# Gated FFN with routed experts: token tiles taken in groups of four, with z and the raw weights held once

## The chip, the cores and the metric

The kernel runs on one core of a Trainium2 chip, as one program. The metric is the device time of one execution in microseconds (us). Three executions of the kernel before took 4530.27, 4531.44 and 4532.99 us, so the median is 4531.44 us.

## What is computed

```python
x = x + tanh(g_xattn[0]) * mixer(ctx, ctx, layernorm(x))      # causal convolution of k v pairs, 64 heads of 8
x = x + tanh(g_ffn[0]) * ffn(layernorm(x))
def ffn(x):                                  # T = 8192 tokens, D = 1024, F = 512, E = 7 experts
    shared = (x1 * silu(x2)) @ shared_w2     # x1, x2 = split(x @ shared_w1)
    aff  = sigmoid(x @ gate_w + expert_bias) # two best experts of a token: mask
    sel  = top_k(where(mask, aff, -1).T, capacity)            # capacity = T // E = 1170 per expert
    out  = _ffn(x[sel], routed_w1, routed_w2) * w             # w = aff where kept, else 0
    return shared + zeros.at[sel].add(out)
```

All of it is in float32. TensorE is fed float32r, whose values are rounded, so each factor is split into a high and a low part, and a product is three matmuls: high x high, high x low, low x high.

## The kernel before, in words

Three blocks follow one another, each behind a barrier. `prepare_filters` is short. `gated_conv` is the mixer: 64 steps, which also leave the normalized tokens in HBM both as rows (`z_d`) and transposed (`zT_d`), the residual in `out`, and the gate's logits in `logit_d`. `experts` is the FFN, and the change touches that block alone. Token tiles are 128 tokens wide for the shared expert (64 tiles) and 117 for a routed one (10 tiles of 117 slots, 7 experts).

**A group is two tiles** (`GS` = 32 shared groups, `GE` = 5 per expert). For each group PE makes the first product (`first_product`, lines 1336 to 1347): for each of four blocks `j` of F and for the two halves of `w1` (value and gate) it sums 8 chunks of D times 3 matmuls, 192 in all, whose moving side is z of the group, 256 or 234 columns. Then comes the second product of the group before (`second_product`, lines 1349 to 1365): for each tile and each half of D 12 matmuls of 512 columns, 48 in all. I call such 12 matmuls a half. An expert's last group is followed by its own second product too (`after`).

Around it, ACT makes Silu of the gate half (`swish`), the high part of the hidden tile (`high`) and of z (`split`); DVE makes the product (`gate_up`), the low parts (`low`, `split`) and takes the results out of PSUM (`result`, line 1266): for the shared expert y = tanh(g) * result + residual, in place in `y[t]`, and for a routed one the result times the weight of its slot. `zh`, `zl`, `hh`, `hl` exist twice, once for each of two groups in turn, so that the z of the next group is split during the first product of this one. PSUM holds `ps1` (two, one bank each), `ps2` (two, one per tile, two banks each) and `psT`.

**Orders written out by hand.** SP issues all loads and stores of the shared part in one queue: per group `load_z(k + 2)`, `store(k - 1)`, `residual(k)` (lines 889 to 892), where a residual waits until the store of the same `y[t]` has landed. POOL gathers a routed tile with an indirect DMA (`gather`, line 948), as rows that PE transposes (`turn`, line 1325), and adds a result tile into `out` with an indirect DMA (`scatter`, line 960), waiting for each to land before the next. Weights come through `raw`, 32 KB per partition: `w1` in four pairs of blocks (`load_pair`), then `w2` in the first half of the same buffer; each is split into high (ACT) and low (DVE) at the turn from one expert to the next (`w1_high`, `w1_low`, `w2_high`, `w2_low`).

**Routing** runs on DVE beside the shared groups. `make_scores` (line 1080) comes first, before the first product may begin. Then the capacity's threshold is searched over 30 bits (`find_bit`), one step in each block `j` of a group; PE adds the counts over the partitions (`tally`). Scans and numbering follow, up to `routed`. POOL then writes (token, weight) of each token's first and second choice into the list in HBM (`scatter_column`, line 928): 64 columns times two indirect DMAs, where each waits for the one before. The list is read back (line 945), and the gathers of the first expert can begin.

## Time and profile before

| | |
|---|---|
| median of 3 executions | 4531.44 us |
| the profiled execution, its own time | 4534.36 us |
| its span, first to last instruction | 4532.4 us |
| PE busy | 4433.4 us (98%), 33098 matmuls |
| PE weight loads busy | 4275.3 us (94%) |
| DVE busy | 2780.8 us (61%) |
| ACT busy | 1492.2 us (33%) |
| POOL busy | 881.7 us (19%) |
| granted PE clock, mean | 0.992 of 2.4 GHz |

The FFN's block begins at 2176.3 us of the span. A matmul's listed length holds its whole way through the array and overlaps with the next one's, so the rate of PE is to be read from the distance of two starts in the timeline. "SPq" is SP's queue of DMA issues; an issue of several DMAs in one row lasts from the first to the last, waits among them. In the groups of instructions, the idle time is that of the engine just before them, with what ended it.

### The profile page before, as it was taken

What the parts mean: (1) busy time and instruction counts of PE and PEld (TensorE: products, weight loads), DVE (VectorE), ACT (ScalarE), POOL (GpSimd) and SP (SyncE); (2) the same over time, 40 slices, a digit from 0 to 9 for tenths busy, and PEclk for the clock granted to TensorE, in tenths of its full rate; (3) what the DMA queues carried; (4) which work ended last, traced back from release to release, by engine and by line L of the source; (5) the groups of instructions that cost most, each with busy time, mean ns of one, the idle gap of its engine ahead of it and who ended that gap; (6) DMA issues with size and microseconds to landing.
All of it is one profiled execution on the core that took longest, in us unless ns stands there. A gap on an engine that the chain in (4) does not pass through costs nothing.

```text
span 4532.4 us, 85207 instructions
## 1 busy us (share of the span) xinstructions
PE 4433.4 (98%) x33098; PEld 4275.3 (94%) x33098; DVE 2780.8 (61%) x3215; ACT 1492.2 (33%) x2179; POOL 881.7 (19%) x1065
## 2 busy tenths in 40 slices
PE   7999999999999999999699999999999999999998
PEld 7999999999999999999599999999999999999997
DVE  7999999999999999998544522222233233233232
ACT  4454554545455454554211111111122122122120
POOL 1222222122221222222000023322111111111211
PEclk9999999999999999999799999999999999999999
DMA  3333333333333333332533344334343443443432
GB/s 106 112 116 106 115 106 110 113 111 116 106 111 106 111 116 109 116 104 86 127 98 88 86 110 117 90 89 99 86 122 78 94 112 70 97 112 70 97 79 39
DMA packets 200325, 457.80 MB, mean 101 GB/s; under 512 B 31434, under 2 KB 97343, under 8 KB 200187
## 3 DMA queue, kind: packets, MB, share of 16 engines
q1 hardware_dynamic: 173515, 388.38, 29.9%
q0 software_dynamic: 26672, 67.34, 7.4%
q8 instruction: 116, 1.90, 0.2%
q14 instruction: 22, 0.18, 0.0%
HBM read 285.80 MB, written 169.83 MB: 101 GB/s over the span
## 4 chain that ended last, share of the span: by engine, by line
PE 50%; DVE 1%; DMA 1%; issue 0%; ACT 0%; POOL 0%; SPq 0%; POOLq 0%; ACTq 0%; DVEq 0%
PE moe_ps L1343 11%; PE moe_ps L1344 11%; PE moe_ps L1345 11%; PE moe_ps L1359 5%; PE moe_ps L1360 5%; PE moe_ps L1361 5%; PE moe_psT L1332 1%; DMA out<-moe_y,moe_add_i 0%; DMA moe_zin<-zT_d 0%; DVE moe_w1l L1232 0%; DVE moe_zl L1245 0%; DVE moe_raw L1146 0%; PE moe_psT L1368 0%; DVE moe_raw L1145 0%; ACT moe_zh L1013 0%
## 5 line engine op out<-in xcount | busy, mean ns | idle before, releaser
L568 PE MATMUL att_psY<-att_kv_hi,att_tz_hi 128*128 128x288 f32 x4608 | 1393.5, 302 | 30.6 <-DVE att_kv_lo L444 30.6
L569 PE MATMUL att_psY<-att_kv_lo,att_tz_hi 128*128 128x288 f32 x4608 | 1359.4, 295 | 0.0
L570 PE MATMUL att_psY<-att_kv_hi,att_tz_lo 128*128 128x288 f32 x4608 | 1355.9, 294 | 0.0
L1343 PE MATMUL moe_ps<-moe_zh,moe_w1h 128*128 128x234 f32 (+1 forms) x4288 | 1205.9, 281 | 30.1 <-DVE moe_zl L1245 25.5
L1344 PE MATMUL moe_ps<-moe_zl,moe_w1h 128*128 128x234 f32 (+1 forms) x4288 | 1199.0, 280 | 3.5 <-issue 3.5
L1345 PE MATMUL moe_ps<-moe_zh,moe_w1l 128*128 128x234 f32 (+1 forms) x4288 | 1198.6, 280 | 0.0
L568 PEld LDWEIGHTS att_psY<-att_kv_hi,att_tz_hi 128*128 128x128 f32 x4608 | 865.4, 188 | 30.6 <-issue 30.6
L570 PEld LDWEIGHTS att_psY<-att_kv_hi,att_tz_lo 128*128 128x128 f32 x4608 | 867.7, 188 | 0.0
L569 PEld LDWEIGHTS att_psY<-att_kv_lo,att_tz_hi 128*128 128x128 f32 x4608 | 867.6, 188 | 0.0
L1343 PEld LDWEIGHTS moe_ps<-moe_zh,moe_w1h 128*128 128x128 f32 x4288 | 824.9, 192 | 34.0 <-issue 31.3
L1344 PEld LDWEIGHTS moe_ps<-moe_zl,moe_w1h 128*128 128x128 f32 x4288 | 825.1, 192 | 6.2 <-issue 4.1
L1345 PEld LDWEIGHTS moe_ps<-moe_zh,moe_w1l 128*128 128x128 f32 x4288 | 825.1, 192 | 0.0
L1024 ACT ACTIVATE moe_act_s<-moe_ps 128x234 f32<-128x234 f32 (+1 forms) x268 | 100.5, 375 | 1744.2 <-PE moe_ps L1345 1744.2
L1258 DVE TENSOR_TENSOR moe_hid<-moe_ps,moe_act_s 128x234 f32<-128x234 f32 (+1 forms) x268 | 110.6, 413 | 886.7 <-ACT moe_act_s L1024 879.7
L343 ACT ACTIVATE att_y<-att_psY 128x576 f32<-128x576 f32 x512 | 333.4, 651 | 860.7 <-PE att_psY L570 858.9
L289 POOL TENSOR_TENSOR att_root<-att_mv,att_eps 128x1 f32<-128x1 f32 x128 | 183.2, 1431 | 1639.8 <-DVE att_mv L434 1560.9
L1359 PE MATMUL moe_ps<-moe_w2h,moe_hh 128*117 128x512 f32 (+1 forms) x1072 | 422.6, 394 | 0.0
L1360 PE MATMUL moe_ps<-moe_w2l,moe_hh 128*117 128x512 f32 (+1 forms) x1072 | 420.6, 392 | 0.0
L1361 PE MATMUL moe_ps<-moe_w2h,moe_hl 128*117 128x512 f32 (+1 forms) x1072 | 420.3, 392 | 0.0
L444 DVE TENSOR_TENSOR att_kv_lo<-att_kv,att_kv_hi 128x2304 fp32r<-128x2304 f32 x128 | 323.5, 2528 | 0.7 <-ACT att_kv_hi L336 0.7
L462 DVE TENSOR_TENSOR att_prod<-att_y,att_qx 128x2048 f32<-128x2048 f32 x128 | 293.6, 2294 | 6.1 <-ACT att_y L343 0.4
L475 DVE TENSOR_TENSOR att_prod<-att_prod 128x2048 f32<-128x2048 f32 x128 | 293.1, 2290 | 2.3
(155 smaller groups left out, 5167.1 us busy)
## 6 DMA issues: line engine op xcount, KB each, us to landing
att_kT<-in_cT SPq DMA_DIRECT2D x64, 512.0 KB, 4.0
att_xn<-in_x SPq DMA_DIRECT2D x64, 512.0 KB, 5.8
att_tz_hi<-filt_hi SPq DMA_DIRECT2D x64, 512.0 KB, 3.8
att_tz_lo<-filt_lo SPq DMA_DIRECT2D x64, 512.0 KB, 4.8
out<-att_x SPq DMA_DIRECT2D x64, 512.0 KB, 4.0
z_d<-att_z SPq DMA_DIRECT2D x64, 512.0 KB, 3.7
zT_d<-att_zT SPq DMA_DIRECT2D x64, 512.0 KB, 4.7
moe_zin<-zT_d SPq DMA_DIRECT2D x64, 512.0 KB
```

What stands on the lines that cost most here:

```text
L343: nc.scalar.activation(y[a // G][:, a % G].rearrange("p (c b) i -> p c (b i)", c=2), psY[a % 2][:, :, 0:NB * PAIRS], ACT.Copy).then_inc(y_ ...
L444: nc.vector.tensor_tensor(kv_lo[u][:, keys_of(half)].rearrange("p t b i -> p (t b i)"), kv[half][:, :, :, :].rearrange("p t b i -> p (t b ...
L462: nc.vector.tensor_tensor(place(0, [HD, D1 + 1], [1, HD]), near, runs(qx[u], half, 0, [1, D1 + 1], [1, HD]), ALU.mult)
L568: nc.tensor.matmul(acc, tz_hi[u][:, d:d + P], hi, start=(c == 0), stop=False)
L569: nc.tensor.matmul(acc, tz_hi[u][:, d:d + P], lo, start=False, stop=False)
L570: last = nc.tensor.matmul(acc, tz_lo[u][:, d:d + P], hi, start=False, stop=(c == a))
L1343: nc.tensor.matmul(acc, w1h[:, c, cols], zh[u][:, c, 0:2 * w], start=(c == 0), stop=False)
L1344: nc.tensor.matmul(acc, w1h[:, c, cols], zl[u][:, c, 0:2 * w], start=False, stop=False)
L1345: last = nc.tensor.matmul(acc, w1l[:, c, cols], zh[u][:, c, 0:2 * w], start=False, stop=(c == C - 1))
L1359: nc.tensor.matmul(acc, hh[u][:, f, rows], w2h[:, f, cols], start=(f == 0), stop=False)
L1360: nc.tensor.matmul(acc, hh[u][:, f, rows], w2l[:, f, cols], start=False, stop=False)
L1361: last = nc.tensor.matmul(acc, hl[u][:, f, rows], w2h[:, f, cols], start=False, stop=(f == FC - 1))
```

## The change

The FFN takes tiles in groups of four in the shared expert (16 groups of 512 tokens) and of four, three and three in a routed one (468, 351 and 351 tokens), so `ps1` becomes two tiles of two banks, and `ps2` one set of two banks instead of two sets. The odd width 351 is rounded up to 352. `zh` and `zl` exist once; a group's z is split after the first product of the group before has ended, in a *window*: there PE makes the second-product halves of the previous group and, in the routed part, turns the tiles of the next one between them, in an order that `window` gives to PE and DVE alike. `zin`, `y`, `hh`, `hl` stay two. `act_s` and `hid` become one each. The gate half of a block is now made before the value half, and Silu starts after it. `raw` is halved to 16 KB per partition: pairs 0 and 1 of `w1` lie in its halves, pairs 2 and 3 follow when 0 and 1 are split. The list exists in two copies, one for each token's first choice and one for its second; each scatter waits only for the previous one of its own copy, and the two are added after they are read back. `make_scores` is done by DVE inside the first group, after block 0, and two routing steps follow each of the blocks 0 to 2 of the next seven groups. The cut diff:

```diff
-    GE = 5
-    M = slots // (2 * GE)
-    TILES = E * 2 * GE
-    GS = H // 2
+    PARTS = (4, 3, 3)
+    PER = sum(PARTS)
+    NG = len(PARTS)
+    M = slots // PER
+    TILES = E * PER
+    GT = 4
+    GS = H // GT
...
+    list_of = [list_d, nc.dram_tensor("list_e", (E * slots + P, 2), I32).ap()]
+    def rows_of(n):
+        return list_of[n][0:E * slots, :].rearrange("(r q) c -> q r c", q=M)
...
-        raw = m.sb("raw", [P, C * F2])
+        raw = m.sb("raw", [P, FC * D])
+        raw1 = [raw[:, q * C * 2 * P:(q + 1) * C * 2 * P].rearrange("p (c b f) -> p c b f", c=C, b=2) for q in range(2)]
...
+        zh = m.sb("zh", [P, C, GT * P], F32R)
+        zl = m.sb("zl", [P, C, GT * P], F32R)
+        act_s = m.sb("act_s", [P, GT * P])
+        hid = m.sb("hid", [P, GT * P])
...
-        ps1 = [m.ps(f"ps1_{j}", [P, 2, 2 * P]) for j in range(2)]
-        ps2 = [m.ps(f"ps2_{t}", [P, 2, BANK]) for t in range(2)]
+        ps1 = [m.ps(f"ps1_{j}", [P, 2, BANK]) for j in range(2)]
+        ps2 = m.ps("ps2", [P, 2, BANK])
...
+        PLACES = [["scores"]] + [STEPS[a:a + EACH] for a in range(0, len(STEPS), EACH)] + [[]]
+        LEAD = len(PLACES)
...
+            lead = [shared(k) for k in range(LEAD)]
+            row(lead, None, shared(LEAD))
+            with eng.Fori(LEAD // 2, GS // 2 - 1) as p:
+                row(pair(2 * p + 1), shared(2 * p)._replace(u=0), shared(2 * p + 3)._replace(u=1))
+            firsts = expert_groups(1, 0)
+            row([shared(GS - 1), *firsts], shared(GS - 2), expert_groups(2, 1)[0])
+            with eng.Fori(0, (E - 3) // 2) as q:
+                both = expert_groups(2 * q + 2, 1) + expert_groups(2 * q + 3, 0)
+                row(both, expert_groups(2 * q + 1, 0)[-1], expert_groups(2 * q + 4, 1)[0])
+            ends = expert_groups(E - 1, 1) + expert_groups(E, 0)
+            row(ends, expert_groups(E - 2, 0)[-1], None)
...
+        def window(prev, nxt):
+            halves = [("half", t, b) for t in range(prev.nt) for b in range(2)] if prev else []
+            tiles = nxt.nt if nxt else 0
+            order = []
+            for a in range(max(len(halves), 1)):
+                order += [("tile", t, None) for t in range(tiles) if t * max(len(halves), 1) // tiles == a]
+                order += halves[a:a + 1]
+            return order
...
+                if j < 2:
+                    wait(sp, w2h_set, FC * n)
+                    wait(sp, w2l_set, FC * n)
+                else:
+                    sp.wait_ge(w1h_set, 2 * FC * n + 2 * (j - 1))
+                    sp.wait_ge(w1l_set, 2 * FC * n + 2 * (j - 1))
...
+            load_z(0, 0)
+            load_pair(0, 0, shared_w1[0])
+            load_z(0, 1)
             sp.dma_start(logit, logit_d).then_inc(logit_in, 16)
             sp.dma_start(g[:, :], g_ffn.rearrange("(a e) -> a e", a=1).to_broadcast([P, 1])).then_inc(const, 16)
-            load_z(0)
-            load_w1(0, shared_w1[0])
-            sp.wait_ge(list_made, 2)
-            sp.dma_start(list_d[0:E * slots, :].rearrange("(r q) c -> q r c", q=M), lists[:, :, :]).then_inc(list_init, 16)
+            load_pair(0, 1, shared_w1[0])
+            load_z(0, 2)
+            load_z(0, 3)
+            load_pair(0, 2, shared_w1[0])
+            load_pair(0, 3, shared_w1[0])
+            load_z(1, 0)
+            load_z(1, 1)
+            sp.wait_ge(list_made, 4)
+            for n in range(2):
+                sp.dma_start(rows_of(n), lists[0][:, :, :].bitcast(I32)).then_inc(list_init, 16)
             load_w2(0, shared_w2[0])
...
             def shared_rows(k):
-                load_z(k + 2)
-                store(k - 1)
-                residual(k)
-            with sp.Fori(1, GR + 4) as k:
+                load_z(k + 1, 2)
+                load_z(k + 1, 3)
+                store(k - 1, 0)
+                residual(k - 1, 2)
+                store(k - 1, 1)
+                residual(k - 1, 3)
+                load_z(k + 2, 0)
+                load_z(k + 2, 1)
+                store(k - 1, 2)
+                residual(k, 0)
+                store(k - 1, 3)
+                residual(k, 1)
...
             def scatter_column(h):
                 for n in range(2):
+                    wait(pool, scattered[n], h * 16)
+                    pool.sem_inc(passed, 1)
                     nc.gpsimd.tensor_copy(stage_i[n][:, :], slot_of[:, bass.ds(h, 1), n:n + 1].rearrange("p a b -> p (a b)")).then_inc(staged, 1)
                     nc.gpsimd.tensor_copy(stage_p[n][:, :], pay[:, bass.ds(h, 1), n, :].rearrange("p a b -> p (a b)")).then_inc(staged, 1)
                     pool.wait_ge(staged, h * 4 + (2 * n + 2))
                     pool.sem_inc(passed, 1)
-                    wait(pool, scattered[1 - n], h * 16 + 16 * n)
-                    pool.sem_inc(passed, 1)
-                    nc.gpsimd.indirect_dma_start(list_d, bass.IndirectOffsetOnAxis(stage_i[n][:, 0:1], 0),
+                    nc.gpsimd.indirect_dma_start(list_of[n], bass.IndirectOffsetOnAxis(stage_i[n][:, 0:1], 0),
                                                  stage_p[n][:, :], None).then_inc(scattered[n], 16)
...
+            for n in range(2):
+                pool.wait_ge(scattered[n], 16 * H)
+                pool.dma_start(lists[n][:, :, :].bitcast(I32), rows_of(n)).then_inc(list_in, 16)
+            pool.wait_ge(list_in, 32)
...
+            def rows(back, ahead, beyond):
+                for t in range(2, ahead.nt if ahead else 0):
+                    gather(ahead, t)
+                for t in range(back.nt if back else 0):
+                    scatter(back, t)
+                for t in range(2 if beyond else 0):
+                    gather(beyond, t)
...
+            def group(prev, cur, nxt):
+                for j in range(FC):
+                    swish(cur, j)
+                    if cur.i == 1 and j == 0:
+                        for c in range(FC):
+                            w2_high(cur, c)
+                    high(cur, j)
+                if nxt:
+                    act.wait_ge(up, FC * cur.k + FC)
+                    for t in range(nxt.nt):
+                        split(nxt, t)
+                        if turnover(cur, nxt) and t == 1:
+                            w1_high(nxt.n, 0)
+                    if turnover(cur, nxt):
+                        for j in range(1, FC):
+                            w1_high(nxt.n, j)
...
+            def group(prev, cur, nxt):
+                places = PLACES[cur.k] if cur.kind == "shared" and isinstance(cur.k, int) and cur.k < LEAD else []
                 for j in range(FC):
-                    gate_up(k, j, w)
-                    if next_kind and j % 2 == 0:
-                        split(k + 1, 1 - u, j // 2, next_kind)
-                    low(k, u, j, w)
-                    if first:
-                        w2_low(n, j)
-                    if places:
-                        route(places[j])
-                if not first:
-                    turnover = next_kind == "routed" and (kind == "shared" or i == GE - 1)
-                    results(k - 1, kind, n + 1, list(range(FC)) if turnover else [])
-            def after_shared():
-                results(GS - 1, "shared", 1, list(range(FC, 2 * FC)))
-                dve.wait_ge(list_in, 16)
-                nc.vector.tensor_scalar(scale[:, :], lists[:, :, 1].bitcast(F32), tg[0:M, 0:1], None,
-                                        ALU.mult).then_inc(scaled, 1)
-                dve.wait_ge(scaled, 1)
-            def after(n, k, u, last):
-                results(k, "routed", n + 1, [] if last else list(range(FC, 2 * FC)))
-            make_scores()
+                    gate_up(cur, j)
+                    low(cur, j)
+                    if cur.i == 1 and j == 0:
+                        for c in range(FC):
+                            w2_low(cur, c)
+                    for step in places[2 * j:2 * j + 2]:
+                        route(step)
+                if cur.kind == "routed" and isinstance(cur.n, int) and cur.n == 1 and cur.i == 1:
+                    weights_listed()
+                turning = turnover(cur, nxt)
+                for what, t, half in window(prev, nxt):
+                    if what == "tile":
+                        split(nxt, t)
+                        if turning and t == 1:
+                            w1_low(nxt.n, 0)
+                        if turning and t == nxt.nt - 1:
+                            w1_low(nxt.n, 1)
+                    else:
+                        result(prev, t, half)
+                if turning:
+                    for j in range(2, FC):
+                        w1_low(nxt.n, j)
...
+                wait(pe, y_set, 2 * (grp.tile + t) + (half - 1))
...
+            def group(prev, cur, nxt):
+                places = PLACES[cur.k] if cur.kind == "shared" and isinstance(cur.k, int) and cur.k < LEAD else []
+                pe.wait_ge(zh_set, cur.tile + cur.nt)
+                pe.wait_ge(zl_set, cur.tile + cur.nt)
+                left = list(places)
                 for j in range(FC):
-                    if isinstance(i, int) and i == 0:
-                        pe.wait_ge(w1h_set, 2 * FC * n + 2 * (j + 1))
-                        pe.wait_ge(w1l_set, 2 * FC * n + 2 * (j + 1))
-                    first_product(k, u, j, w)
-                    if places and j > 0:
-                        sum_partitions(places[j - 1])
-                    if next_kind == "routed" and j % 2 == 0:
-                        turn(k + 1, j // 2)
-                if not (isinstance(i, int) and i == 0):
-                    if i == 1:
-                        pe.wait_ge(w2h_set, FC * n + FC)
-                        pe.wait_ge(w2l_set, FC * n + FC)
-                    second_product(k - 1, 1 - u, w, places[FC - 1] if places else None)
-            def after_shared():
-                second_product(GS - 1, 1, P)
-            def after(n, k, u, last):
-                second_product(k, u, M)
+                    if cur.i == 0:
+                        pe.wait_ge(w1h_set, 2 * FC * cur.n + 2 * (j + 1))
+                        pe.wait_ge(w1l_set, 2 * FC * cur.n + 2 * (j + 1))
+                    wait(pe, gated, FC * cur.k + (j - 1))
+                    for b in (1, 0):
+                        first_product(cur, j, b)
+                        if j > 0 and left:
+                            sum_partitions(left.pop(0))
+                for what, t, half in window(prev, nxt):
+                    if what == "tile":
+                        if nxt.kind == "routed":
+                            turn(nxt, t)
+                    else:
+                        second_product(prev, t, half)
```

`first_product(grp, j, b)` now makes one half `b` of a block with the group's width, `second_product(grp, t, half)` one half. `load_z(k, t)` waits for `zh_set` and `zl_set` to reach 4k + t - 1, `residual(k, t)` for the last store of `y[t % 2]`. At the end SP stores groups 14 and 15 of the shared part without z loads ahead, and loads pairs 2 and 3 and `w2` of the first expert between them. POOL calls `rows` once per group.

## Rows read from the trace of the kernel before

**Rows 1.** Busy time in stretches: length, PE busy, granted clock, DMA share, GB/s

```profile
2176.29:2199.10 22.81, 0.00 (x0) 0.50 1.10 242
2199.10:2253.93 54.83, 50.43 (x387) 0.90 0.60 116
2719.96:2787.80 67.84, 67.84 (x482) 1.00 0.52 124
3314.79:3486.30 171.51, 171.51 (x1282) 1.00 0.38 90
4491.80:4532.40 40.60, 22.84 (x101) 0.82 0.31 48
```

**Rows 2.** Groups of PE matmuls by line and shape: busy, mean ns, idle

```profile
L1343 PE MATMUL moe_ps<-moe_zh,moe_w1h 128*128 128x234 f32 x2240 | 622.7, 278 | 0.2 <-issue 0.2
...
L1343 PE MATMUL moe_ps<-moe_zh,moe_w1h 128*128 128x256 f32 x2048 | 583.2, 285 | 29.9 <-DVE moe_zl L1245 25.5 <-DVE moe_hid L1258 4.4
```

**Rows 3.** Timeline of PE, first product of two shared tiles: start, length

```profile
2699.89 0.28 PE L1343 MATMUL moe_ps<-moe_zh,moe_w1h 128*128 128x256 f32 x1
...
2701.33 0.28 PE L1343 MATMUL moe_ps<-moe_zh,moe_w1h 128*128 128x256 f32 x1
```

**Rows 4.** Timeline of PE, second product of a shared tile

```profile
2744.67 0.39 PE L1361 MATMUL moe_ps<-moe_w2h,moe_hl 128*128 128x512 f32 x1
...
2745.58 0.39 PE L1359 MATMUL moe_ps<-moe_w2h,moe_hh 128*128 128x512 f32 x1
```

**Rows 5.** Timeline of PE, first product of two routed tiles

```profile
3319.81 0.27 PE L1343 MATMUL moe_ps<-moe_zh,moe_w1h 128*128 128x234 f32 x1
...
3320.70 0.27 PE L1345 MATMUL moe_ps<-moe_zh,moe_w1l 128*128 128x234 f32 x1
```

**Rows 6.** Timeline of PE: the first product of the FFN begins

```profile
2199.11 0.55 PE L1343 MATMUL moe_ps<-moe_zh,moe_w1h 128*128 128x256 f32 x1 [25.46 <-DVE moe_zl L1245]
```

**Rows 7.** Chain that ended last, from 2170 us: start, length, what

```profile
2206.36 12.21 DMA moe_zin<-zT_d
2218.59 1.06 ACT moe_zh L1013
2219.68 1.23 DVE moe_zl L1245
```

**Rows 8.** Timeline of DVE: last step of the scores

```profile
2193.62 0.62 DVE L1118 SCALAR_TENSOR_TENSOR moe_score<-moe_y,moe_score 128x448 f32<-128x448 f32 x1
```

**Rows 9.** Timeline of DVE, results of a shared group

```profile
2748.50 0.75 DVE L1271 SCALAR_TENSOR_TENSOR moe_y<-moe_ps,moe_tg,moe_y 128x512 f32<-128x512 f32 x1 [1.87 <-PE moe_ps L1361]
```

**Rows 10.** Timeline of the SP queue, stores and residual loads

```profile
2754.72 0.58 SPq L875 DMA_DIRECT2D out<-moe_y  x1
...
2760.60 0.58 SPq L870 DMA_DIRECT2D moe_y<-out  x1
...
2822.75 0.59 SPq L875 DMA_DIRECT2D out<-moe_y  x1
...
2827.96 0.59 SPq L870 DMA_DIRECT2D moe_y<-out  x1
```

**Rows 11.** DMA issues of the page: count, KB each, us from issue to landing

```profile
att_tz_hi<-filt_hi SPq DMA_DIRECT2D x64, 512.0 KB, 3.8
att_tz_lo<-filt_lo SPq DMA_DIRECT2D x64, 512.0 KB, 4.8
...
moe_zin<-z_d,moe_get_i POOLq DMA_INDIRECT x70, 4.7
```

**Rows 12.** Timeline of POOL: first scatter of the list, then loading the list

```profile
2610.67 0.19 POOL L930 COPY moe_stage_i<-moe_slot_of 128x1 int32<-128x1 int32 x1 [432.86 <-DVEq L1226]
...
3189.09 3.41 POOL L945 DMA_DIRECT2D moe_lists<-list_d  x1 [2.24 <-DMA list_d<-moe_stage_p,moe_stage_i]
```

**Rows 13.** Timeline of POOL at the end: scatters of results

```profile
4499.84 1.59 POOL L968 DMA_INDIRECT out<-moe_y,moe_add_i  x1 [0.86 <-POOL moe_add_i L965]
...
4507.50 1.57 POOL L968 DMA_INDIRECT out<-moe_y,moe_add_i  x1 [0.86 <-POOL moe_add_i L965]
```

More of the change, by code:

```diff
@@ new lines, in experts, with shared @@
+        STEPS = list(range(BITS)) + ["compare", "scan ties", "scan ties on", "keep", "scan kept", "scan kept on",
+                                     "number", "first", "second", "weigh", "no second", "no first"]
+        EACH = 2 * (FC - 1)
+        PLACES = [["scores"]] + [STEPS[a:a + EACH] for a in range(0, len(STEPS), EACH)] + [[]]
+        LEAD = len(PLACES)
+        assert LEAD == 9 and GS >= LEAD + 3 and (GS - 1 - LEAD) % 2 == 0
+        def shared(k):
+            return Grp("shared", k, GT * k, 0, GT, k % 2 if isinstance(k, int) else None, 0, k if isinstance(k, int) else 2)
@@ new lines, in routed_group, with expert_groups, schedule, row @@
+        def routed_group(n, k0, u0, i):
+            at = sum(PARTS[:i])
+            return Grp("routed", k0 + i, PER * (n - 1) + (H + at), at, PARTS[i], (u0 + i) % 2, n, i)
+        def expert_groups(n, u0):
+            return [routed_group(n, NG * (n - 1) + GS, u0, i) for i in range(NG)]
+        def schedule(eng, group):
+            def row(groups, before, behind):
+                chain = [before, *groups, behind]
+                for a in range(1, len(chain) - 1):
+                    group(chain[a - 1], chain[a], chain[a + 1])
+            def pair(k):
+                return [shared(k)._replace(u=1), shared(k + 1)._replace(u=0)]
+            lead = [shared(k) for k in range(LEAD)]
[9 more added lines that the diff above has]
+            row(ends, expert_groups(E - 2, 0)[-1], None)
@@ new lines, in rows, with around @@
+            def rows(back, ahead, beyond):
[5 more added lines that the diff above has]
+                    gather(beyond, t)
+            def around(groups, before, behind):
+                chain = [before, *groups, *behind]
+                for a in range(1, len(groups) + 1):
+                    rows(chain[a - 1], chain[a + 1], chain[a + 2])
@@ new lines, in after_next @@
+            def after_next(n):
+                return expert_groups(n + 1, 0)[0:2]
+            one = expert_groups(1, 0)
+            gather(one[0], 0)
+            gather(one[0], 1)
+            rows(None, one[0], one[1])
+            rows(None, one[1], one[2])
+            for t in range(2):
+                pool.wait_ge(stored[t], 16 * (GT // 2 * GS))
+            two = expert_groups(2, 0)
+            rows(one[0], one[2], two[0])
+            rows(one[1], two[0], two[1])
+            with pool.Fori(2, E) as n:
+                around(expert_groups(n, 0), expert_groups(n - 1, 0)[-1], after_next(n))
@@ L988, in _ @@
+            zero = shared(0)
+            split(zero, 0)
+            w1_high(0, 0)
+            for t in range(1, GT):
+                split(zero, t)
+            for j in range(1, FC):
+                w1_high(0, j)
             act.wait_ge(const, 16)
@@ L1055, in after_shared @@
-            def after_shared():
-                act.wait_ge(up, FC * GS)
-                w1_high(1)
-            def after(n, k, u, last):
-                if not last:
-                    act.wait_ge(up, FC * (k + 1))
-                    w1_high(n + 1)
-            split(0, 0, 0, "shared")
-            split(0, 0, 1, "shared")
-            w1_high(0)
-            schedule(act, group, after_shared, after)
+            schedule(act, group)
         @block.vector
@@ L1427, in build @@
+            pe.wait_ge(made, 2)
+            schedule(pe, group)
+            last = expert_groups(E, 0)[-1]
+            for t in range(last.nt):
+                for half in range(2):
+                    second_product(last, t, half)
 def build(nc, x, xT, cT, g_xattn, g_ffn, ssm_kernel, D, gate_w, expert_bias, shared_w1, shared_w2,
```

525 lines of the change are left out of this document (247 added, 278 removed).

## Prediction

> **What bounds the kernel now.** I began with the busy shares (PE 98%, DVE 61%, in the table above), then asked for stretches, since a share is a mean over two stages. Inside the FFN, PE is busy for the whole of a stretch of two shared groups (67.84 of 67.84 us) and of a whole expert (171.51 of 171.51) [rows 1]: no wait ends last there, so only shorter PE work can gain, and every new PE wait costs its full length. PE idles only around the edges: 25.5 us before the first product of the FFN and 4.4 us before its second group [rows 2], and at the end, where the last 40.6 us hold 22.84 us of PE work [rows 1].
>
> What does a matmul cost? Its listed length (278, 285 ns) overlaps the next, so I took the distance between starts. At 256 columns 12 starts take 1.44 us, 120.0 ns each [rows 3]; at 512 columns 4 take 0.91, 227 ns [rows 4]; at 234 columns 8 take 0.89, 111 ns [rows 5]. Columns at the granted 2.4 GHz explain 106.7, 213.3 and 97.5 ns. What is left is 13.3, 13.9 and 13.8 ns: a cost **per matmul**, whatever its width. The 512-column row is the second product; it is the only one of the width that the first product is to get.
>
> **First products.** Before, they are 3 x (2240 + 2048) matmuls [rows 2]. After, 16 shared groups and 21 routed ones, 192 each.
> - Shared, four tiles: before, the row of 67.84 us [rows 1]. After, 192 x 0.227 = 43.6 us and 96 second-product matmuls x 0.227 = 21.8 us: 65.4. Saved 2.4 x 16 = 39 us.
> - Routed, an expert: before 960 x 0.1113 = 106.8 us. After, 192 x (468/2.4 + 13.8 = 208.8 ns) = 40.1 us and 384 x (352/2.4 + 13.8 = 160.5 ns, as 351 is rounded up to 352) = 61.6: 101.7. Saved 5.1 x 7 = 36 us. Second products and transposes keep their number.
> Together **-75 us**.
>
> The Trainium skill (TensorE: Matmul & The Clock Gate, Back-to-back issue gap) gives N/2.4 + 2.5 ns for one matmul after another. That rule speaks against this change: by it 5760 fewer matmuls save 14 us, not 75. The rows above disagree at all three widths, and I go by them.
>
> **Start of the FFN, +5.** Scores leave the way of the first product, but four tiles of z must now be split before it. SP orders z, a pair of w1, z, the second pair, then z 2 and 3, each into a buffer that the split of z 0 or 1 frees. Counting 512 KB every 1.8 us behind the first landing near 2180 (an estimate from the landings around this stretch), the last z is there near 2194; ACT's and DVE's split take 1.06 and 1.23 us [rows 7], and PE starts at about 2196.5 instead of 2199.1 [rows 6]: -2.6. The scores took until 2194.2, 18 us after the stage began at 2176.3 [rows 1, 8]; now they run on DVE from 13 us into group 0, whose product lasts 44 us. They hold back the gate of block 1 until 31 us; block 3 asks for it at 33. Hidden, with 2 us to spare.
> Then a new hole: zh and zl exist once, so no split of group 1 can begin before group 0's product ends, there are no halves of a previous group to cover it, and z 2 and 3 are loaded only into freed buffers. Last gate and high 1.6 us, split of z 0 2.3: 3.9; load of z 2 4 to 5 (512 KB took 3.8, and 4.8 as the second of two [rows 11]); split of z 2 2.3, then that of z 3, which lands 2 us later. About 12.5 us idle, and 2 more at the lower clock level after it: this stage shows 0.50 granted while PE is idle and 0.90 in the stretch after [rows 1]. Against this stand the old 4.4 us hole and its own slow matmuls: 54.83 us for 384 matmuls of 120 ns, 46.1: 8.7 [rows 1]. Old offset 2199.1 + 8.7; new 2196.5 + 2 + 12.5 + 2: +5. The list is now written twice at the start, and behind the single write a z load took 12.2 us [rows 7]; by my count both writes and w2 are through at about 2246, when z 2 is asked for. So I allow up to +15, and down to 0.
>
> **Routing steps, +2.5.** Two steps now lie in a block of 10.9 us, as one did in 5.8. Four parts of w2l (1.23 us each, the size of the split [rows 7]) go in front of the first one: PE waits 3.3 us once. The tie scan holds PE about 1 us, and its old two stalls (under 2 us together) go, which takes 0.8 off. 0 to +6.
>
> **The shared window, +25.** This is my largest unknown. With PE at T (end of a group's product), PE makes eight halves of 2.72 us; y has two buffers for four tiles. So tile 2's first result needs: tile 0 stored, then its residual loaded. In SP's order two z loads stand ahead of that store, the second one waiting for the split of z 1, which DVE does after result 1. Result 1 ends 6.25 us after T (two halves, then 0.75 [rows 9]), the split of z 1 at 7.5, the second z load goes out, and the store at 7.9. Store to freed buffer, from the second store of a pair to the load that waits for it: 5.9 and 5.2 us [rows 10]; I take 5.1 from seven such pairs. Then the load, 3.9: 16.9; result 0.75 and semaphores 0.3: 18.1. PE wants to start half 6 at 16.3, and ps2 is one set, so half 6 waits for this result. PE loses 1.8 us. Who is behind: half 7, then the next group's product; z 3's split, at about 20, isn't later than that. Windows of that kind: groups 1 to 14, 14 x 1.8 = **25 us**. With 3.8 for both transfers next to nothing is lost; with 5.9 for both 4.3 us each, 60 us.
>
> **Routed windows, +4.** Here y is freed by scatters, 7.66 us from one to the next [rows 13]. The first goes out at about T + 8.6, tile 2's result comes at 15.5, tile 3's at 21.4 while its buffer is free at 22.5; PE waits only for results two halves back, so it isn't held. A gather goes out 1.1 us after its buffer is freed and takes 4.7 [rows 11]; tile 3 is turned 8 us later at the nearest. POOL's chain is 2 gathers, 4 scatters and 2 gathers, some 45 us in a 4-tile window of 55. Turn 1 waits for z 0's split about 0.2 us: 21 x 0.2 = 4. A new expert's w1 comes through two buffers: pair 0 is split by T + 9.5 (needed 20), pair 3 by 28 (needed 50). Cover if that fails: none. Bounds 0 and +15.
>
> **Lists, 0.** The old chain took 578 us for 128 scatters, 4.5 each [rows 12], every one waiting for the last. Two lists let one run beside the other; I reckon 6 us per pair, so 380 us. Routing now ends near 2700 instead of 2610, the lists are there near 3100, and the first turn asks for its gather near 3245. Price 0 as long as those 145 us last.
>
> **End, +4.** From the last product's end (2 matmuls into the last stretch) to the end of the program it is 40.3 us, for 22.3 us of halves [rows 1]. Now 6 scatters follow instead of 4: 40.3 + 2 x 7.66 = 55.6, for 33.5 us of halves. Overhang 22 instead of 18.
>
> **Sum.** -75 + 5 + 2.5 + 25 + 4 + 4 = -34.5. The profiled execution took 4534.4 us (span 4532.4): 4499.9. The median shown is 2.9 below it: **4497 us**.
>
> **Rivals.**
> - *The residuals come in time.* For it: 3.8 us is the shorter landing of the pair [rows 11], and the z load ahead may be over sooner. Then -25: 4472. Against: the second of two takes 4.8 there, and stores 5.2 and 5.9 [rows 10]. Chance 0.16.
> - *The residual chain costs its upper end*, as list scatters run beside it: 14 x 4.3 = 60 instead of 25: 4532, no change. 0.10.
> - *The list becomes the bound (slower).* If the two lists' scatters serialise after all in POOL's DMA queue, they take 578 us from 2700, loading both lists 33 more and a gather 6: turn 0 of the first expert at 3317 instead of 3245, and nothing else is there for PE. +72: 4569. It decides from about 7.9 us per pair (506 us for 64 pairs) against the old 9.0. For it: both lists go through POOL's one software queue. Against: 128 entries of 8 bytes are little to move, so most of the 4.5 us must be the way to completion, which two can share. 0.08.
> - *The change doesn't save per matmul*: wide first products would need more than their columns plus 13.8 ns, with only some 14 us gained: 4558. The second product at the same width speaks against it. 0.02.
> - Some wait that I don't see, of over 25 us: 0.08, mostly slower.
> The forecast keeps 0.56.
>
> **How the numbers follow.** A measurement of this kernel tells 0.2%, 9 us, from no change. Below 4522: forecast, first rival and a part of the second and last, 0.76; within 9 us 0.11; slower 0.13. The range takes the unknown costs' bounds: low 4497 - 25 - 5 - 4 = 4463; high 4497 + 35 + 8 = 4540, which leaves out the list case.
>
> **What would show it.** Distances of 227, 209 and 160 ns between first-product starts show the saving. In groups 1 to 14, PE idle before line-wise the second product of tile 2 or 3, put down to DVE's result and that to the residual's DMA, 1 to 3 us each, shows the window; none would show the first rival. One PE hole of 12 us between groups 0 and 1; POOL's last list scatter before 3120; six scatters 7.7 us apart at the end. PE idle before the first transposes in the list case. The forecast is wrong if idle time in the shared windows is near 0 or near 60 us, or if expert periods exceed 167 us by more than 1.

## The result: 4556.7 us, slower by half a per cent, and the profile after

| | before | after |
|---|---|---|
| median | 4531.44 us | 4556.7 us |
| lowest and highest of 5 runs | 4529.17 and 4534.48 | 4553.46 and 4557.42 |
| span of the profiled execution | 4532.4 us | 4555.4 us |
| PE busy | 4433.4 us, 33098 matmuls | 4385.9 us, 27338 matmuls |
| granted PE clock, mean | 0.992 | 0.984 |

The ratio is 1.0054, with a 95% interval of 1.0042 to 1.0065. The forecast was 4497 us, in a range of 4463 to 4540: the change was slower than all of it. PE is busy 47 us less, and the time still grew by 25.

**What came as forecast.** Two stretches of the changed kernel (length, then busy time of PE, PE weight loads, DVE, ACT and POOL, then granted clock, DMA share, GB/s). The first is one expert and answers to the 171.51 us of [rows 1]; the second holds two shared windows.

```profile
3520.10:3686.41 166.31, 166.31 (x897) 148.44 (x896) 53.45 (x66) 32.96 (x46) 31.58 (x40) 1.00 0.41 96
2720.00:2860.00 140.00, 128.91 (x550) 105.69 (x549) 39.67 (x61) 17.31 (x23) 52.73 (x117) 0.96 0.33 90
```

An expert takes 166.31 us, 5.2 less than before; 5.1 were forecast. In the shared part PE is no longer busy throughout: 128.91 of 140 us, at a clock of 0.96 instead of 1.00. Now the groups of PE matmuls, first product and then second product, each shared and routed (count, busy, mean ns, idle time before them), which answer to [rows 2]:

```profile
L1440 PE MATMUL moe_ps<-moe_zh,moe_w1h 128*128 128x512 f32 x1024 | 403.9, 394 | 33.4 <-DVE moe_zl L1338 21.8 <-issue 11.5
L1440 PE MATMUL moe_ps<-moe_zh,moe_w1h 128*128 128x352 f32 x896 | 289.3, 323 | 0.0
L1458 PE MATMUL moe_ps<-moe_w2h,moe_hh 128*128 128x512 f32 x512 | 213.0, 416 | 62.8 <-DVE moe_y L1365 62.8
L1458 PE MATMUL moe_ps<-moe_w2h,moe_hh 128*117 128x512 f32 x560 | 225.5, 403 | 3.3 <-DVE moe_y L1370 3.3
```

The hole between groups 0 and 1 is the 11.5 us of the first row (about 12.5 forecast). The new entry is 62.8 us ahead of the shared second product, ended by DVE's `result` (line 1365). DVE's own waits show that this line waits for a DMA (us in total, times, longest):

```profile
DVE moe_y L1365 <- DMA moe_y<-out: 183.2, 32, 9.7
```

It is one wait per window, 14 of them, always before half 6, the first half of tile 3: it needs the bank of PSUM that half 4 filled, and DVE can't empty that one before tile 2's residual is there. Three of the 14 in PE's timeline (in brackets the idle time): a typical one, the longest, and the last, which is also the shortest.

```profile
2398.25 0.50 PE L1458 MATMUL moe_ps<-moe_w2h,moe_hh 128*128 128x512 f32 x1 [3.56 <-DVE moe_y L1365]
...
2912.44 0.80 PE L1458 MATMUL moe_ps<-moe_w2h,moe_hh 128*128 128x512 f32 x1 [7.01 <-DVE moe_y L1365]
...
3273.23 0.79 PE L1458 MATMUL moe_ps<-moe_w2h,moe_hh 128*128 128x512 f32 x1 [2.94 <-DVE moe_y L1365]
```

What the first of these three is made of shows in the chain that ended last (start, length, what), here from the split of z 1 on. PE's product of the group had ended at 2378.1, which is the T of the prediction.

```profile
2384.52 1.23 DVE moe_zl L1338
...
2386.60 4.96 DMA out<-moe_y
...
2391.72 5.63 DMA moe_y<-out
...
2397.45 0.76 DVE moe_y L1365
...
2398.25 0.50 PE moe_ps L1458
```

The store goes out at T + 8.5 (7.9 forecast) and takes 5.0 (5.1 forecast); the residual load takes 5.6, not 3.9. The same two rows of the longest wait, which stands beside the list scatters:

```profile
2897.35 8.05 DMA out<-moe_y
...
2905.56 6.05 DMA moe_y<-out
```

Over the 14 windows the load takes 5.6 to 6.1 us in the eight away from the scatters and 5.7 to 6.6 in the six beside them; the store takes 4.4 to 5.4 and 5.9 to 8.1. Beside the scatters it is mainly the store that grows.

After the wait PE is slow for a while. These stretches of the typical window show it: the clock column falls from 1.00 to 0.71 and returns.

```profile
2384.00:2388.00 4.00, 4.00 (x20) 3.30 (x19) 2.49 (x3) 1.06 (x1) 0.00 (x0) 1.00 0.56 181
2396.00:2400.00 4.00, 1.75 (x6) 1.37 (x7) 2.54 (x3) 0.00 (x0) 0.00 (x0) 0.87 0.32 100
2400.00:2404.00 4.00, 4.00 (x14) 3.22 (x13) 0.38 (x1) 0.00 (x0) 0.00 (x0) 0.71 0.93 259
2404.00:2408.00 4.00, 4.00 (x20) 3.28 (x19) 1.12 (x2) 0.00 (x0) 0.00 (x0) 1.00 0.71 263
```

PE's timeline there gives the price. Two starts at the lower level (1.2 GHz), and two once the clock is back at 2.4 GHz:

```profile
2399.56 0.63 PE L1459 MATMUL moe_ps<-moe_w2l,moe_hh 128*128 128x512 f32 x1
2399.99 0.63 PE L1460 MATMUL moe_ps<-moe_w2h,moe_hl 128*128 128x512 f32 x1
...
2402.70 0.40 PE L1458 MATMUL moe_ps<-moe_w2h,moe_hh 128*128 128x512 f32 x1
2402.93 0.40 PE L1459 MATMUL moe_ps<-moe_w2l,moe_hh 128*128 128x512 f32 x1
```

Starts lie 0.43 us apart instead of 0.23, over some eight matmuls. I call *excess* what the distances of all starts in the 8 us behind a wait have above 0.227 us, summed: 1.75 us here, 1.44 to 2.78 in the 14 windows, 26.4 us together. About 0.12 us of each is there also behind a short wait at full clock (below), so the clock costs 25 us. **A window wait thus costs its idle time and about 1.8 us more: 62.8 + 24.7 = 87.5 us where 25 were forecast.** That surplus of 62.5 us is about the whole miss (60 us in the medians).

My theory then: the residual chain is longer than forecast, and each wait lowers the clock as well. Rivals: the list scatters beside it, a fixed cost of the wider groups, contention inside the chain.

### The profile page after: what moved, and what is told of

The parts are those of the page before. It is cut to its first block, busy times and chain, and to the rows that moved or that the text cites. A ratio compares the mean times of both kernels' runs of the same rounds, so it can differ in the third digit from the quotient of the medians.

```text
span 4555.4 us, 71624 instructions
## 1 busy us (share of the span) xinstructions
PE 4385.9 (96%) x27338; PEld 4059.9 (89%) x27338; DVE 2749.4 (60%) x2975; ACT 1463.4 (32%) x1939; POOL 877.1 (19%) x1072
## 4 chain that ended last, share of the span: by engine, by line
PE 45%; DMA 5%; DVE 1%; issue 1%; SPq 0%; ACT 0%; POOL 0%; DVEq 0%; POOLq 0%
PE moe_ps L1440 10%; PE moe_ps L1441 10%; PE moe_ps L1442 10%; PE moe_ps L1458 4%; PE moe_ps L1460 4%; PE moe_ps L1459 4%; DMA moe_y<-out 2%; DMA out<-moe_y 2%; PE moe_psT L1429 1%; DMA out<-moe_y,moe_add_i 1%; DVE moe_zl L1338 0%; DVE moe_y L1365 0%; DMA moe_zin<-zT_d 0%; DMA moe_raw<-in_L_ffn_shared_w 0%; SPq L896 0%
## 5 line engine op out<-in xcount | busy, mean ns | idle before, releaser
L1440 PE MATMUL moe_ps<-moe_zh,moe_w1h 128*128 128x512 f32 (+2 forms) x2368 | 860.5, 363 | 33.6 <-DVE moe_zl L1338 21.8
L1441 PE MATMUL moe_ps<-moe_zl,moe_w1h 128*128 128x512 f32 (+2 forms) x2368 | 858.9, 363 | 0.0
L1442 PE MATMUL moe_ps<-moe_zh,moe_w1l 128*128 128x512 f32 (+2 forms) x2368 | 856.6, 362 | 0.0
L1351 DVE TENSOR_TENSOR moe_hid<-moe_ps,moe_act_s 128x512 f32<-128x512 f32 (+2 forms) x148 | 91.7, 619 | 897.4 <-PE moe_ps L1442 874.6
L1440 PEld LDWEIGHTS moe_ps<-moe_zh,moe_w1h 128*128 128x128 f32 x2368 | 446.0, 188 | 85.9 <-issue 34.6
L1458 PE MATMUL moe_ps<-moe_w2h,moe_hh 128*117 128x512 f32 (+1 forms) x1072 | 438.5, 409 | 66.1 <-DVE moe_y L1365 62.8
L1442 PEld LDWEIGHTS moe_ps<-moe_zh,moe_w1l 128*128 128x128 f32 x2368 | 447.8, 189 | 51.4
L1441 PEld LDWEIGHTS moe_ps<-moe_zl,moe_w1h 128*128 128x128 f32 x2368 | 446.4, 189 | 50.8 <-issue 0.2
L1122 ACT ACTIVATE moe_act_s<-moe_ps 128x512 f32<-128x512 f32 (+2 forms) x148 | 79.9, 540 | 818.9 <-PE moe_ps L1442 818.9
L1127 ACT ACTIVATE moe_hh<-moe_hid 128x512 fp32r<-128x512 f32 (+2 forms) x148 | 85.3, 576 | 707.9 <-DVE moe_hid L1351 707.9
L1458 PEld LDWEIGHTS moe_ps<-moe_w2h,moe_hh 128*117 128x117 f32 (+1 forms) x1072 | 202.3, 189 | 121.3 <-DVE moe_y L1365 68.9
```

What stands on the lines that cost most here:

```text
L1440: nc.tensor.matmul(acc, w1h[:, c, cols], zh[:, c, 0:w], start=(c == 0), stop=False)
L1441: nc.tensor.matmul(acc, w1h[:, c, cols], zl[:, c, 0:w], start=False, stop=False)
L1442: last = nc.tensor.matmul(acc, w1l[:, c, cols], zh[:, c, 0:w], start=False, stop=(c == C - 1))
L1458: nc.tensor.matmul(acc, hh[grp.u][:, f, rows], w2h[:, f, cols], start=(f == 0), stop=False)
```

## Experiments

Each changes the changed kernel; times are medians beside runs of the kernel before on the same chip (4530.66, 4533.4 and 4534.25 us in the three sets), and "saved" is against 4556.7.

### The first store ahead of the second z load

```diff
                 load_z(k + 1, 2)
-                load_z(k + 1, 3)
                 store(k - 1, 0)
+                load_z(k + 1, 3)
                 residual(k - 1, 2)
...
```

The same order is given to the last groups of the shared part.

> Theory: in the windows of groups 1 to 14 PE waits for tile 2's result, which waits for the residual's load, which waits for the store of tile 0; that store stands in SP's queue behind the second z load and goes out 8.5 us after the group's product ends. With the store ahead of that z load it goes out at 6.4, so PE's idle time before half 6 falls from 3.2-7.0 us by about 2.1 us in each of 14 windows (62.8 us of idle to about 33), and where what is left is short the slow matmuls behind the wait may go too: 4500 to 4527 us. Rival (PE waits because ps2 is one set, whatever SP does): no change, 4550 to 4560.

4504.1 us (4497.76 to 4508.32), ratio 0.9935 (0.9921 to 0.9948). PE's waits, and two of them in its timeline, before and during the list scatters:

```profile
PE moe_ps L1459 <- DVE moe_y L1366: 27.0, 14, 3.4
```
```profile
2596.46 0.50 PE L1459 MATMUL moe_ps<-moe_w2h,moe_hh 128*128 128x512 f32 x1 [1.41 <-DVE moe_y L1366]
...
2809.25 0.80 PE L1459 MATMUL moe_ps<-moe_w2h,moe_hh 128*128 128x512 f32 x1 [3.43 <-DVE moe_y L1366]
```

The sum of waits falls by 36 us, but 53 us are saved. The rest is the clock: behind the eight waits of 0.82 to 1.41 us the excess is 0.12 to 0.16 us, so the clock stayed up; behind the six of 2.12 to 3.43 us it is 1.7 to 2.9. Waits and excess together are 40.7 us instead of 89.2, 48.5 us less; the two profiled executions differ by 48.9. One store moved in SP's order turns the change from slower to faster.

### The list without its scatters

```diff
             scatter_column(0)
-            with pool.Fori(1, H) as h:
-                scatter_column(h)
...
```

This leaves out 63 of the 64 columns of the list, so most slots of the routed experts carry no token.

> Leaves out 63 of the 64 columns of the list, so nearly all slots hold nobody and the routed part works on empty rows. Theory: the small scatters of the list lengthen the store and the load beside them, so the idle time in the windows between 2740 and 3130 us (4.3 to 7.0 us) falls to the 3.2 to 3.8 of the other windows: 15 us less idle in all, some 4535 to 4543. Rival (those windows are longer because of the loop over registers, or a growing backlog in SP's queue): no change there, 4550 to 4560.

4551.57 us (4549.78 to 4553.06), ratio 1.0043 (1.0028 to 1.0059): 5 us saved, less than expected and within the rival's range; its interval overlaps that of the changed kernel, so the traces must decide. The waits fall to 53.5 us. In the first window past the one column, while the lists are read back, the wait is 5.7 us; from the next on the waits are 2.9 to 3.9 us, as in the windows that had no scatters before. The loop or a backlog in SP's queue, the rival, would have kept them long. One of them:

```profile
2909.46 0.50 PE L1456 MATMUL moe_ps<-moe_w2h,moe_hh 128*128 128x512 f32 x1 [3.71 <-DVE moe_y L1363]
```

So the scatters do lengthen the residual chain. But the shorter waits still lower the clock, and the excess even grew, from 26.4 to 30.5 us. Idle plus excess fell by 5.2 us, about what was saved. The list is a part of the miss, and the smaller one.

### Filler in front of half 6

```diff
+                        if prev.kind == "shared" and t == 3 and half == 0:
+                            pe.wait_ge(gated, FC * cur.k + FC)
+                            for a in range(FILLER):
+                                nc.tensor.matmul(ps1[0][:, 0, 0:HALF], w2h[:, a % FC, 0:P], w2h[:, a % FC, 0:HALF],
+                                                 start=(a == 0), stop=(a == FILLER - 1))
```

16 useless matmuls a window, 3.6 us, stand where PE would idle. All 16 windows with second products of a shared group get them, the 14 with a wait and two that have none.

> Adds 16 matmuls of 512 columns (3.6 us of PE work whose result nobody reads) in front of half 6 of each shared window. Theory: the second half of the loss is the clock, 1.2 instead of 2.4 GHz for some 4 us behind each wait, 2 us a window. With PE busy through the wait the clock stays up: the windows that waited 3.2 to 3.8 us get 1.5 to 2 us shorter although PE does more, the others less; 4525 to 4548. Rival (only the wait costs, the clock reading is a by-product): the same time or up to 10 us more, 4555 to 4567.

4543.87 us (4539.23 to 4545.1), ratio 1.0026 (1.0016 to 1.0036): PE does 58 us more work (256 matmuls) and the kernel is 13 us **faster**. The shared stretch says why (960 us, from 2320); first this kernel, then the changed one:

```profile
2320.00:3280.00 960.00, 946.15 (x4154) 777.93 (x4153) 290.72 (x503) 118.09 (x159) 182.94 (x394) 0.99 0.33 93
```
```profile
2320.00:3280.00 960.00, 896.08 (x3841) 733.45 (x3840) 289.50 (x500) 116.44 (x156) 185.62 (x394) 0.96 0.33 91
```

Work in place of waiting kept the clock at 0.99 instead of 0.96. Waits of 12.7 us and 5.6 us of excess are left. With the 58.1 us of filler that makes 76.4 us instead of 89.2, 12.8 less, and 12.8 us are saved: 51 us of the filler stand in the place of 50 us of idle time, the 7 us in the two other windows are simply added, and the clock gives back 21.

### Stores and residuals by halves of a tile

```diff
-            def residual(k, t):
-                wait(sp, stored[t % 2], 16 * (GT // 2 * k + t // 2))
-                sp.dma_start(y[t % 2][:, :], o_rows[GT * k + t]).then_inc(res_in[t % 2], 16)
+            def residual(k, t, b):
+                cols = slice(b * HALF, (b + 1) * HALF)
+                wait(sp, stored[t % 2][b], 16 * (GT // 2 * k + t // 2))
+                sp.dma_start(y[t % 2][:, cols], o_rows[GT * k + t][:, :, cols]).then_inc(res_in[t % 2][b], 16)
...
+            def first_round(k, then=None, after=None):
+                store(k, 0, 0)
+                store(k, 0, 1)
+                if then:
+                    then()
+                residual(k, 2, 0)
+                store(k, 1, 0)
+                residual(k, 2, 1)
```

`store` waits for its half's result alone, and `then` is the z load.

> Stores and residuals of the shared part go by halves of a tile (256 KB), each with its own semaphore, so that tile 2's first residual can be asked for 4 us earlier and takes less time; the number of bytes is the same. Theory: no wait of PE is left in the windows of groups 1 to 14, neither the 62.8 us of idle nor the about 28 us of low clock: about 4466 us, 4455 to 4485, with shared groups of 65.4 to 67 us. Rival 1 (the wait is only moved, to SP's queue of twice as many issues or to z): 4500 or more. Rival 2 (wide products don't save what the prediction says): not below 4500 even with no waits in the windows.

4466.4 us (4463.09 to 4467.73), ratio 0.9854 (0.9839 to 0.987), faster than both kernels. The window waits are gone but for one (the second product, and the same stretch as above):

```profile
L1468 PE MATMUL moe_ps<-moe_w2h,moe_hh 128*128 128x512 f32 x512 | 201.2, 393 | 0.8 <-DVE moe_y L1375 0.8
```
```profile
2320.00:3280.00 960.00, 958.07 (x4262) 792.41 (x4261) 318.33 (x532) 134.19 (x179) 192.60 (x402) 1.00 0.36 103
```

90 us saved, where idle and excess were 89.2 and 0.9 are left: the account closes, and no fixed cost of the wider groups is left over. PE's busy time is 4359.3 us here, 74 less than before, where 75 were forecast for the first products. How much of the gain is the earlier request and how much the shorter transfer was not separated.

### The same, with the wide matmuls cut in two

```diff
+                pieces = [(0, w // 2), (w // 2, w)] if grp.kind == "shared" else [(0, w)]
+                for lo, hi in pieces:
+                    acc = ps1[j % 2][:, b, lo:hi]
```

> The kernel with stores and residuals by halves of a tile (4466 us in its own runs, 0.9854 of before), and in the 16 shared groups each first-product matmul of 512 columns made as two of 256, so 3072 matmuls more over the same columns. If a matmul costs its columns at 2.4 GHz and 13.3 ns on top, as the starts 120.0 ns apart at 256 columns and 227 ns at 512 say: +41 us, 4507 us, starts 120 ns apart, a shared group's product 46.1 us instead of 43.6. The Trainium skill (TensorE: Matmul & The Clock Gate, Back-to-back issue gap) gives 2.5 ns in place of 13.3; by that +8 us, 4474 us. Rival: the 13 ns belong to the way from one accumulation to another or to the weight loads that are shared, then under +20 us.

4509.58 us (4504.25 to 4511.5), ratio 0.9947 (0.9933 to 0.996): 43 us more than without the cut, over 3072 matmuls 14.1 ns each (13.7 by the ratios, since the two ran in different sets). Their starts are 120 ns apart, as in [rows 3]:

```profile
2699.11 0.28 PE L1455 MATMUL moe_ps<-moe_zh,moe_w1l 128*128 128x256 f32 x1
2699.23 0.28 PE L1453 MATMUL moe_ps<-moe_zh,moe_w1h 128*128 128x256 f32 x1
```

The saving that the change was to bring is real, and is not the part that failed. The estimate by the Trainium skill's 2.5 ns (TensorE: Matmul & The Clock Gate, Back-to-back issue gap) gave +8 us; the measurement decides against it for this stream. The section gives that figure for the gap of isolated matmuls, without the weight loads that this stream has beside each.

### The residual load alone on the DMA engines

```diff
                 residual(k - 1, 2)
+                sp.wait_ge(res_in[0], 16 * (GT // 2 * (k - 1) + 1) + 16)
                 store(k - 1, 1)
```

> The changed kernel (4557 us), in which SP lets the store of tile 1 go out only when the residual of tile 2 has landed, so that this load has the DMA engines to itself. Theory: the 5.6 us of the load are contention with the store issued 0.9 us behind it. Then it takes about 3.9 us, the PE wait before the second product of tile 2 falls by 1.7 us in each of 14 windows (3.1 to 3.8 us become 1.5 to 2.1, the sum 63 becomes about 39), and the time is about 4533 us, or lower if the clock stays up after shorter waits. Tile 3's residual lands some 9 us after tile 2's result, behind which DVE has nothing that PE asks for at once. Rival: a residual load takes 5.6 us in itself, or the wait comes from the store; then the waits stay at 60 us and the time at 4555 to 4560.

4550.77 us (4539.66 to 4554.87), ratio 1.0034 (1.0021 to 1.0048). **My theory of contention fell.** The chain in one window:

```profile
2382.18 4.32 DMA out<-moe_y
...
2386.67 5.18 DMA moe_y<-out
```

With no store of SP behind it the load takes 5.2 us here, and 5.2 to 6.0 over the 14 windows, 5.45 in the mean where it was 5.90; 3.9 had been expected. So contention with that store is worth about 0.45 us, and the rest the load takes by itself. (The expectation names the place of the wait loosely: it stands before tile 3's product, for tile 2's result.) The waits add up to 57.9 us and the excess to 24.2, 7 us less together: about what 14 loads of 0.45 us less can give. The time alone would not tell it from the changed kernel, as the intervals overlap.

### z of group 1 loaded early

On the kernel with halves: z of tiles 2 and 3 of group 1 goes into the two `y` buffers during group 0, since the residuals aren't needed yet.

```diff
+        def z_from(grp, t):
+            at = y if isinstance(grp.k, int) and grp.k == 1 and t >= 2 else zin
+            return at[t % 2][:, :]
...
-            for t in range(2):
-                for b in range(2):
-                    residual(0, t, b)
             load_z(1, 2)
             load_z(1, 3)
             load_z(2, 0)
             load_z(2, 1)
+            for t in range(2):
+                for b in range(2):
+                    residual(0, t, b)
```

> The kernel with stores and residuals by halves of a tile (4466 us), with z of tiles 2 and 3 of group 1 loaded during group 0 into the two y buffers, whose residuals come afterwards. It takes away the load out of the hole of 11.6 us between groups 0 and 1. Theory: what is left is the last gate and high part, and four splits of 1.23 us each on DVE, 7.4 us; so 4.2 us less, 4462 us. Rival: the two residuals, now loaded at the start of group 1, are no later than the first window needs them; if they are, a wait there gives the gain back (4466).

4462.32 us (4462.06 to 4464.06), ratio 0.9844 (0.983 to 0.9857): 4 us less, the best kernel of this study. The intervals of the two overlap; the trace shows the gain. The hole is 7.16 us, where it was 11.6:

```profile
2249.39 0.77 PE L1458 MATMUL moe_ps<-moe_zh,moe_w1h 128*128 128x512 f32 x1 [7.16 <-issue]
```

### The same, with one chain of list scatters

```diff
-                    wait(pool, scattered[n], h * 16)
+                    wait(pool, scattered[1 - n], h * 16 + 16 * n)
```

> The kernel with halves and with z of group 1 loaded early (4462 us), with one part of the change undone: each scatter of the list waits for the one before it in either copy, as in the kernel before. There 128 scatters took 578 us (4.5 each); here the two copies side by side took 375 us (2700.5 to 3075), the first gather went out at 3177 and the first transposes began at 3228. Theory: a scatter is mostly waiting for completion, which two copies share. Then the chain ends at 3279, the list is ready 28 us later at 3307, the first transposes come at 3313, and PE idles about 85 us before them: 4547 us, slower than the kernel before. Rival: what limits the scatters is the queue or POOL itself and the two copies bring nothing that this order takes away; then the time stays near 4462 us.

4583.06 us (4577.05 to 4585.09), ratio 1.0106 (1.0089 to 1.0123): slower than every other kernel here. From POOL's timeline the first copy, then the read of the first list; and PE's first transposes:

```profile
2698.11 0.19 POOL L1018 COPY moe_stage_i<-moe_slot_of 128x1 int32<-128x1 int32 x1 [520.31 <-DVEq L1335]
...
3312.50 3.42 POOL L1030 DMA_DIRECT2D moe_lists<-list_d  x1
```
```profile
3346.84 1.82 PE L1447 MATMUL moe_psT<-moe_ident,moe_zin 117*128 117x117 f32 x8 [120.60 <-DMA moe_zin<-z_d,moe_get_i]
```

128 scatters take 614 us, 4.8 each, since the staging copies now wait as well; two chains side by side took 375. PE idles 120.6 us, and 120.7 are lost (85 expected). This order is stricter than that of the kernel before, where the staging copies did not wait and one chain took 578 us; by the expectation's estimate that alone would leave 85 us of idle time and 4547 us. So without the two copies of the list this order of the work would be slower than the kernel before. POOL's one queue doesn't serialise the scatters: a pair side by side takes 5.9 us (375 / 64) where one alone takes 4.8, so most of a scatter's time is waiting that two can share.

## Why the prediction was wrong, step by step

- **What bounds the kernel** (PE without waits, so each new one costs its length): right, but incomplete. A wait cost more than its length.
- **First products, -75:** right. 166.31 us per expert (166.4 by the forecast), 65.28 us per shared group where no wait is left (65.4; the distance of two groups' first starts in the kernel with z loaded early), and 14.1 ns per matmul in the kernel with the cut matmuls.
- **Start of the FFN, +5:** right. PE begins at 2196.30 (2196.5 forecast), the hole is 11.5 us (12.5).
- **Routing steps, +2.5:** right in its waits: the tally waits 2.7 us once (3.3), the ranking 1.1. But behind the 2.7 us the clock falls as well, 1.7 us of excess.
- **The shared window, +25: the step that failed.** The mechanism, its place and its 14 windows were as told; the size was 87 us.
  - (a) "Then the load, 3.9": it was 5.6 to 6.1 in the quiet windows, those away from the list scatters, and 5.45 in the mean with no store behind it. I had taken the loads of filters in the mixer as the nearest rows [rows 11]. The page of the kernel before also listed, one line above them, the load of x, tiles of tokens as rows as the residual is, at 5.8 us; that row I passed over. With it the wait comes to 1.8 + 1.9 = 3.7 us, 52 us in all; the eight quiet windows have 2.9 to 4.3, 3.5 in the mean, which is 48 for 14. That the layout is the reason for the long load is argued and not tested; the store of the same layout on that page, 4.0 us, would have been too low for the 4.4 to 5.4 of the quiet windows. (The chain's terms add up to 17.95 and not 18.1, so 1.65 us a window, and 4.45 at the upper end.)
  - (b) In the six windows beside the list scatters the waits are 4.9 to 7.0 us, 35 together, 14 more than six quiet ones, mainly as the store takes 5.9 to 8.1 us there, not 5.1. I had priced the lists at 0 because they were in time, which they were, and not for what they do to other transfers.
  - (c) The clock. I charged 2 us for it behind the hole at the start, and nothing behind the 14 waits: 25 us.

  My upper bound of 60 for the window all but covers (a) and (b), with 62.8 us of idle time, but not (c). The prediction had named idle time near 60 us in the shared windows as the sign that it was wrong.
- **Routed windows, +4:** no wait of that kind shows, so 4 us too much. **Lists, 0:** in time; 384 us of scatters (380). **End, +4:** 57.0 us from the last product to the end (55.6), 1.4 more: the six scatters set it, 7.5 to 7.9 us apart but once 9.5.

Together: -34.5, + 62.5 for the windows, + 1.7 for the clock behind the tally, - 4, + 1.4, gives +27; measured +25 in the medians and +23 in the profiled executions. The last few microseconds stay open. Of the rivals, "the residual chain at its upper end" came nearest, and it too was 25 us low, for (c). "The list becomes the bound" did not happen, though the last experiment shows that one chain in place of two would have been enough for it.

## What to carry to other kernels

When buffers of a store-and-reload chain are fewer than the tiles of a group, write out the whole chain in the queue's order, and price each transfer by the row of the same tensor layout (here the load's came out and the store's was low); then ask what stands ahead of the store in its queue. A wait of PE that recurs can be charged twice, once as idle time and once as slow matmuls behind it: shortening waits of some 3.5 us to 1.2 us saved the 2.3 us of each and 1.6 us of excess besides. Halving the transfer of such a chain (store and reload by halves) took the wait away for no memory.

## What was unexpected of the hardware

- Behind every window wait of 2.94 to 7.01 us the granted clock was at its lower level (1.2 GHz) for some 3 to 6 us, and in the kernel with the first store ahead it stayed at 2.4 GHz behind eight waits of up to 1.41 us. No single length divides the two: with the residual load alone it stayed up behind a wait of 2.52 us and fell behind one of 2.47, and with the first store ahead it fell behind 2.12. At the end of the changed kernel it stayed up behind 3.00 us, with the next starts 0.33 and 0.23 us apart:

```profile
4530.04 0.49 PE L1458 MATMUL moe_ps<-moe_w2h,moe_hh 128*117 128x512 f32 x1 [3.00 <-DVE moe_y L1370]
4530.37 0.40 PE L1459 MATMUL moe_ps<-moe_w2l,moe_hh 128*117 128x512 f32 x1
4530.60 0.40 PE L1460 MATMUL moe_ps<-moe_w2h,moe_hl 128*117 128x512 f32 x1
```

- Filler work of 58 us made a kernel 13 us faster.
- At the lower level the 512-column starts are 427 ns apart, which is the columns alone; the 13.9 ns on top of them show only at the higher level.
- A residual load of 512 KB takes 5.6 to 6.1 us with a store running behind it and 5.2 to 6.0 without, away from the list scatters. Beside the scatters the store before it takes 5.9 to 8.1 us, away from them 4.4 to 5.4 (both in the changed kernel).
- Two chains of dependent scatters on one queue ran 1.6 times as fast as one (375 us against 614), and 1.5 times as fast as the one chain of the kernel before (578).
